# First attention: groups of four heads, one score matmul per block, rough scores by parts of a PSUM bank, and a new order of work

## The chip, the core and the metric

One core of a Trainium2 chip runs the whole kernel in one launch. The metric is the device time in microseconds (us), as the median of several runs. Engines are named TensorE (PE, with its weight loads PEld), VectorE (DVE), ScalarE (ACT), GpSimd (POOL) and SyncE (SP), which only issues DMAs here.

## The reference

Two transformer layers on x (2 x 512 x 128) with a context of 154 rows: an attention with 16 heads of 8, a mixture of experts that picks tokens per expert, a masked attention over the context, and a mixture of experts with 32 experts. Only the first attention is touched. Its input is the layer-normed x, its keys and values come from the context, and it has no mask:

```python
q = (query @ Wq.T + bq).reshape(b, tq, 16, 8).transpose(0, 2, 1, 3)
k = (key @ Wk.T + bk).reshape(b, tk, 16, 8).transpose(0, 2, 1, 3)
v = (value @ Wv.T + bv).reshape(b, tk, 16, 8).transpose(0, 2, 1, 3)
scores = jnp.einsum('bhqd,bhkd->bhqk', q, k) / np.sqrt(8)
attn = jax.nn.softmax(scores, axis=-1)
out = jnp.einsum('bhqk,bhkd->bhqd', attn, v)
out = out.transpose(0, 2, 1, 3).reshape(b, tq, 128)
return out @ Wo.T + bo
```

After it come x1 = x + attention, the gate's scores of x1 (8 experts) and a search for each expert's 128th largest score.

## The kernel before, in words

The kernel is written without a scheduler: each engine has one list of instructions, in the order of the program text, and every hand-over is a semaphore (`wait_ge` ahead of an instruction, `then_inc` behind one). An engine whose next instruction waits does nothing else meanwhile. PSUM has eight banks of 512 float columns, and the text assigns them by hand.

The first attention runs over four combinations c of a batch half b = c // 2 (512 queries) and a half g = c % 2 of the heads (eight heads, 64 rows). The queries and keys stand as rows: keys of a combination are spread over 2 x 616 columns (four heads x 154 keys each, padded to 640), where a head's rows are nonzero only in its own columns (`expand`, by GpSimd, L322, the first by VectorE, L459). So one matmul over 128 key columns scores several heads at once, and 10 blocks of 128 columns make a combination.

For the float precision that is wanted, a query q and a key k are split into high and low parts of type fp32r. The rows are q high and q low (`qa`) against k high twice (`ka`), and q high against k low (`kb`, `qb`). The last rows of `kb` and `qb` hold an indicator of the head (loaded by a DMA of its own, `ind`, and cast at L852) and minus the row maximum, so that the block comes out of PSUM ready for the exponential. A block is thus two matmuls (L1152, 128 rows, and L1153, 72 rows) and one exponential on ScalarE (L868), written into a ring of 8 tiles (`pT`).

The row maximum comes from rough scores (high parts of the keys only), computed ahead: for each tile i of 128 queries, `rough` (L1122) fills three banks (0 to 2; for the first combination 3 to 5 as well) with 512 + 512 + 232 columns, and VectorE reduces 2 x 4 heads x 154 columns at once (L474). `maxima` on TensorE turns the four tiles of maxima (L1047), and ScalarE writes minus the maxima (L815).

`queries(c)` is a full-precision projection into bank 6 (L1088, two passes of 512 columns); ScalarE copies it twice (L801 and L802) and VectorE takes the low part (L465). Bank 6 is also used by `turned`, `values`, `back_turned` and `project`, one after the other. `attend(c, r)` (L1166), r = 0 to 2, multiplies four blocks with the values, as four 32-column groups side by side. `outputs` copies the result (L826), `out_turned` turns it (L1047), `normalise` divides (L487, L488), `back_turned` and `project` (L1209) bring it to x1 (L496). `gate_turn` and `logits` (L1226) begin the gate; `gate_shift` on VectorE (L513 to L520) and `gate_exp` on ScalarE (L841) follow.

The order on TensorE is a loop over c and the ten blocks: score block i, then whatever is due at that i (a rough tile at i = 1, 3, 5, 7 for the next combination, an attend at i = 5, and so on); after the tenth block attend 1, maxima of c + 1, queries of c + 2 and attend 2. In the last combination `logits(0)` stands at i = 8, ahead of attends 1 and 2. ScalarE's list has, behind the last exponential, `gate_exp(0)` and then the two halves of `outputs(3)`. Between them TensorE does matmuls without use (`early_work`, L1066, and `idle_work`, L1053). GpSimd's expansions of combinations 2 and 3 wait for all scores of the combination two before, whose columns they overwrite.

Of the kernel before, what the change touches and what calls it, by code (L numbers as in the profile page):

```python
# [27 lines left out]
COMBOS = 2 * B  # L28
E0, F0 = 8, 512
# [7 lines left out]
for _u in range(PAIRS):  # L37
    STEPS.append((_u, 1))
    if _u + 3 < PAIRS:
# [6 lines left out]
ROUGH_AT = (1, 3, 5, 7)  # L46
ORDER = (0, 3, 5, 8, 1, 4, 6, 9, 2, 7)
ROUNDS = (((0, 0, 0), (1, 1, 1), (2, 0, 2), (3, 1, 3)),
          ((0, 1, 4), (1, 2, 5), (2, 1, 6), (3, 2, 7)),
          ((0, 2, 8), (1, 0, 8), (2, 2, 9), (3, 0, 9)))  # L50
# [18 lines left out]

PACK = {}  # L70
_at = 0
for _name, _width in (("ident", P), ("headmask", HH), ("bq", 2), ("bk", 2), ("vmask", 6 * 2 * DH), ("vones", 6 * 2 * DH), ("tri", P), ("group", P),
                      ("iota", P), ("jf", len(SHIFTS)), ("jg", EXACT + 1), ("cand0", 1), ("bo", D), ("bv", 1),
                      ("ln_w", 1), ("ln_b", 1), ("bd_s", 1), ("b1", E0 * FT), ("esel", E0), ("row", 1)):
    PACK[_name] = (_at, _at + _width)
    _at += _width
# [4 lines left out]
def build(nc, x_d, ctx2_d, mask_d, watt_d, ind_d, pack_d, rows_d, gate_d, fc1_d, fc2_d, wout_d, wr_d, rec_d,  # L81
          bd_d, out_d):
    with ExitStack() as ctx:
# [31 lines left out]
        watt = sb("watt", [P, 6, D])  # L115
# [18 lines left out]
        qa, qb, ka, kb = lay(arena_a, ([P, 2, S], [P, 2, S], [P, 2, NBLK * P], [P, 2, NBLK * P]))  # L134
# [10 lines left out]
        ind = pT[HW:HW + HH, :, :].rearrange("p a b -> p (a b)")[:, 0:NBLK * P]  # L145
# [32 lines left out]
        kT = sb("kT", [P, 2, B, SK])  # L178

        arena_e = sb("arena_e", [P, 2 * E0 * D], F32R)  # L180
        khi, klo = lay(arena_e, ([P, 2, B, SK], [P, 2, B, SK]))
        ohi, olo = lay(arena_e, ([P, E0, D], [P, E0, D]))
        smax = sb("smax", [P, COMBOS * TB, HH])
# [45 lines left out]
        L = {n: sem("ld_" + n) for n in ("x0", "x1", "ctx2", "watt", "pack", "late", "rows", "gate", "fc1", "fc2", "mask", "wout", "wr", "bd", "ind")}  # L229
        names = """var_ready rstd_ready consts_ready xn_ready xnT_psum xnT_ready q_psum qhi_ready qlo_ready k_psum  # L230
        kT_ready khi_ready klo_ready ka_first kb_ind expanded v_psum vraw_ready vaug_ready rough_done max_done twice_var twice_ready
# [21 lines left out]
        def heads(v):  # L253
            return v.rearrange("p (q c) -> p q c", q=2)[:, :, 0:HALF].rearrange("p q (h k) -> p q h k", h=HH // 2)

        def own_heads(rows):
            return const("headmask")[0:rows, :].rearrange("p (q h) -> p q h", q=2)[:, :, :, None]\
                .broadcast_to([rows, 2, HH // 2, SK])
# [3 lines left out]
        def _(sp):  # L262
            sp.dma_start(x[:, 0:TB], x_d[:, 0:TB]).then_inc(L["x0"], 16)
            sp.dma_start(watt[:, 0:4], watt_d[:, 0:4]).then_inc(L["watt"], 16)
            sp.dma_start(watt[:, 4:], watt_d[:, 4:]).then_inc(L["late"], 16)
# [23 lines left out]
        def _(pool):  # L289
# [23 lines left out]
            pool.wait_ge(Z["pad_zero"], 2)  # L313
            expansions = [0]

            def expand(dst, src, c, rows):

                b, g = c // 2, c % 2
                expansions[0] += 1
                if expansions[0] > 1:  # L320
                    pool.wait_ge(Z["expanded"], expansions[0] - 1)
                pool.tensor_tensor(heads(dst[0:rows, c % 2, :]),  # L322
                                   f32(src[0:rows, g, b, None, None, :]).broadcast_to([rows, 2, HH // 2, SK]),
                                   own_heads(rows), ALU.mult).then_inc(Z["expanded"], 1)
# [12 lines left out]

            pool.wait_ge(Z["klo_ready"], 1)
            expand(kb, klo, 0, HW)
            expand(ka, khi, 1, P)  # L340
            expand(kb, klo, 1, HW)
            pool.wait_ge(Z["expanded"], 3)
            pool.wait_ge(L["late"], 48)
            values(0)
            rsqrt()
            indicators(pool.tensor_copy, 1)
            for c in range(2, COMBOS):
                pool.wait_ge(Z["score_psum"], (c - 1) * NBLK)
                expand(ka, khi, c, P)
                expand(kb, klo, c, HW)  # L350
                if c == 2:
                    values(1)
                    pool.wait_ge(L["x0"], 16)
                    pool.wait_ge(L["x1"], 16)
                    pool.tensor_tensor(x1[:, :, :], x[:, :, :], const("bo")[:, None, :].broadcast_to([P, T, D]),
                                       ALU.add).then_inc(Z["xbo_ready"], 1)
# [50 lines left out]
        def _(dve):  # L407
# [40 lines left out]
            def norm(src, dst, t0, done):  # L448
# [5 lines left out]
            dve.wait_ge(Z["kT_ready"], 2)  # L454
            dve.tensor_copy(khi[:, :, :, :], kT[:, :, :, :]).then_inc(Z["khi_ready"], 1)
            dve.wait_ge(Z["khi_ready"], 1)
            dve.tensor_tensor(klo[:, :, :, :], kT[:, :, :, :], f32(khi[:, :, :, :]), ALU.subtract)\
                .then_inc(Z["klo_ready"], 1)
            dve.tensor_tensor(heads(ka[:, 0, :]), f32(khi[:, 0, 0, None, None, :]).broadcast_to([P, 2, HH // 2, SK]),  # L459
                              own_heads(P), ALU.mult).then_inc(Z["ka_first"], 1)  # L460

            def q_lo(c):

                dve.wait_ge(Z["qhi_ready"], 2 * c + 2)
                dve.scalar_tensor_tensor(qa[HW:P, c % 2, :], bank[HW:P, 6, :], const("bq")[HW:P, c % 2:c % 2 + 1],  # L465
                                         f32(qa[HW:P, c % 2, :]), ALU.add, ALU.subtract)\
                    .then_inc(Z["qlo_ready"], 1)

            def maxima(c, i):

                n = c * TB + i
                c0 = 3 * 512 * (i % 2) if c == 0 else 0
                dve.wait_ge(Z["rough_done"], n + 1)
                dve.tensor_reduce(smax[:, n, :].rearrange("p (q h) -> p q h", q=2), heads(flat[:, c0:c0 + NBLK * P]),  # L474
                                  AX.X, ALU.max).then_inc(Z["max_done"], 1)
# [22 lines left out]
            q_lo(0)  # L498
            for i in range(TB):
                maxima(0, i)  # L500
            dve.wait_ge(L["x1"], 16)
            norm(x, xn, TB, "xn_ready")
            dve.wait_ge(L["late"], 48)
            dve.tensor_copy(trib[:, :], const("tri")).then_inc(Z["consts_ready"], 1)
            dve.tensor_copy(groupb[:, :], const("group")).then_inc(Z["consts_ready"], 1)

# [27 lines left out]

            q_lo(1)
            for c in range(COMBOS):
                if c + 1 < COMBOS:
                    for i in range(TB):
                        if c and i == 2:
                            normalise(c - 1)  # L540
                        maxima(c + 1, i)
                    if c + 2 < COMBOS:
                        q_lo(c + 2)
# [235 lines left out]
        def _(act):  # L779
# [71 lines left out]
            for n in range(2):  # L851
                act.copy(kb[HW:HW + HH, n, :], ind).then_inc(Z["kb_ind"], 1)  # L852
            act.wait_ge(L["late"], 48)
            indicators(act.copy, 0)
            for r in range(2):
                values(0, r)
# [834 lines left out]
```

## Time and profile before

| what | value |
|---|---|
| median of 3 runs | 281.58 us (281.22 to 281.99) |
| the profiled execution | 282.88 us |
| its span, first to last instruction | 281.1 us |
| mean granted clock of TensorE | 0.961 |
| busy: PE, PEld, DVE, ACT, POOL | 245.8, 168.1, 180.1, 133.4, 72.5 us |

The profiled execution is one run with the hardware profiler; the trace's times count from the span's start, and 1.8 us lie around the span. A matmul's busy time runs to the modelled end of its results, so neighbours overlap; the distance between starts is what TensorE's queue pays.

### The profile page before, as it was taken

The page shows a single profiled execution, that of the slowest core. Times are in us where ns is not written, and L with a number is a line of the kernel's source. Part 1 is how long each engine was busy: PE and PEld are TensorE (multiplying, and loading weights), DVE is VectorE, ACT ScalarE, POOL GpSimd, SP SyncE. Part 2 cuts the span into 40 slices and gives each one's busy share as a digit, 9 for nine tenths or more (in the row PEclk, how much of TensorE's full clock was granted, in tenths as well). Part 3 has the DMA queues.
Part 4 walks back from the last instruction along what each step waited for, and adds up shares of the span by engine and source line. Part 5 has one row for each costly group of instructions (what it writes and reads, how often), then busy time and mean ns, then how long its engine had stood idle before and what let it go on. Part 6 is the DMA issues. An engine that isn't in the chain of part 4 may idle for free.

```text
span 281.1 us, 3672 instructions
## 1 busy us (share of the span) xinstructions
PE 245.8 (87%) x1244; PEld 168.1 (60%) x1244; DVE 180.1 (64%) x416; ACT 133.4 (47%) x268; POOL 72.5 (26%) x103
## 2 busy tenths in 40 slices
PE   8886998989987666999999768788879999999993
PEld 3454545455644213678788537666558888888872
DVE  3695445363455886677245173688888888888883
ACT  2544364645632940252434233766555555555551
POOL 4572060920305300000192030030023535353200
PEclk9999899999999797799999986999999999999998
DMA  7980000000000000000043000000002121210001
GB/s 244 426 336 3 2 0 0 1 2 1 2 0 0 0 0 2 1 0 0 2 92 100 0 0 0 2 0 1 0 2 61 51 71 44 75 39 0 2 0 75
DMA packets 5156, 11.52 MB, mean 41 GB/s; under 512 B 809, under 2 KB 1929, under 8 KB 4882
## 3 DMA queue, kind: packets, MB, share of 16 engines
q1 hardware_dynamic: 4290, 10.47, 11.3%
q10 hardware_dynamic: 848, 0.82, 0.9%
q8 instruction: 10, 0.16, 0.3%
q14 instruction: 8, 0.07, 0.1%
HBM read 10.77 MB, written 0.52 MB: 40 GB/s over the span
## 4 chain that ended last, share of the span: by engine, by line
PE 65%; DVE 16%; issue 7%; ACT 6%; POOL 5%; DVEq 0%; ACTq 0%; POOLq 0%
PE bank L1517 5%; PE bank L1521 5%; PE bank L1518 5%; PE bank L1047 4%; PE bank L1122 3%; DVE att L571 3%; PE bank L1550 3%; PE bank L1393 3%; PE bank L1066 3%; DVE smax L474 3%; PE bank L1403 3%; PE bank L1547 3%; PE bank L1166 2%; PE bank L1530 2%; PE bank L1548 2%
## 5 line engine op out<-in xcount | busy, mean ns | idle before, releaser
L1012 ACT ACTIVATE arena_d<-bank,bias 128x512 f32<-128x512 f32 x34 | 23.4, 688 | 32.9 <-PE bank L1521 32.9
L868 ACT ACTIVATE arena_c<-bank 128x512 f32<-128x512 f32 x40 | 23.0, 598 | 23.0 <-PE bank L1153 22.9
L474 DVE TENSOR_REDUCE smax<-bank 128x8 f32<-128x1232 f32 x16 | 22.8, 1439 | 15.6 <-PE bank L1122 15.6
L736 DVE SCALAR_TENSOR_TENSOR arena_d<-bank,bias,arena_d 128x512 f32<-128x512 f32 x34 | 25.5, 750 | 10.3 <-ACT arena_d L1012 10.0
L1517 PE MATMUL bank<-arena_b 128*128 128x512 f32 x68 | 27.0, 397 | 0.3 <-DVE arena_d L745 0.3
L1521 PE MATMUL bank<-arena_b 128*128 128x512 f32 x68 | 26.6, 390 | 0.0
L1518 PE MATMUL bank<-arena_b 128*128 128x512 f32 x68 | 26.5, 390 | 0.0
L391 POOL CAST arena_b<-rec 128x512 fp32r<-128x512 f32 x17 | 13.7, 808 | 48.7 <-PE bank L1550 48.6
L297 POOL TENSOR_TENSOR rstd<-vareps,neghalf 128x4 f32<-128x4 f32 x8 | 8.1, 1010 | 62.5 <-DVE vareps L433 62.5
L750 DVE TENSOR_TENSOR arena_a<-arena_d,arena_a 128x512 fp32r<-128x512 f32 x34 | 23.4, 689 | 0.7 <-ACT arena_a L1019 0.7
L633 DVE TENSOR_SCALAR arena_a<-bank,pack 128x512 fp32r<-128x512 f32 x16 | 12.0, 751 | 17.0 <-PE bank L1385 16.9
L1019 ACT CAST arena_a<-arena_d 128x512 fp32r<-128x512 f32 x34 | 20.8, 611 | 3.6 <-DVE arena_d L745 2.3
L745 DVE TENSOR_TENSOR arena_d<-arena_d,bank 128x512 f32<-128x512 f32 x32 | 21.8, 680 | 0.8 <-PE bank L1530 0.8
L322 POOL TENSOR_TENSOR arena_a<-arena_e,pack 64x1232 fp32r<-64x1232 f32 (+1 forms) x7 | 16.7, 2392 | 17.6 <-PE bank L1153 13.4
L1053 PE MATMUL bank<-pack,onesb 128*128 128x512 bf16 x69 | 19.6, 429 | 0.0
L1122 PE MATMUL bank<-arena_a 128*128 128x512 f32 (+1 forms) x48 | 13.8, 400 | 5.8 <-DVE smax L474 3.2
L1152 PE MATMUL bank<-arena_a 128*128 128x512 f32 x40 | 18.3, 458 | 0.3 <-ACT arena_c L868 0.2
L394 POOL TENSOR_TENSOR arena_b<-rec,arena_b 128x384 fp32r<-128x384 f32 x17 | 16.4, 962 | 1.4
L1122 PEld LDWEIGHTS bank<-arena_a 128*128 128x128 f32 x48 | 8.2, 196 | 14.1 <-DVE smax L474 7.2
L1153 PE MATMUL bank<-arena_a 72*128 72x512 f32 x40 | 16.1, 402 | 0.0
L1550 PE MATMUL bank<-arena_a,arena_b 128*128 128x512 f32 x34 | 13.8, 407 | 2.3 <-DVE arena_a L750 2.2
L1517 PEld LDWEIGHTS bank<-arena_b 128*128 128x128 f32 x68 | 12.8, 188 | 3.5 <-DVE arena_d L745 0.7
(247 smaller groups left out, 517.9 us busy)
## 6 DMA issues: line engine op xcount, KB each, us to landing
rec<-in_rec SPq DMA_DIRECT2D x17, 257.0 KB, 2.7
arena_d<-in_fc SPq DMA_DIRECT2D x1, 2048.0 KB, 11.0
fc<-in_fc SPq DMA_DIRECT2D x1, 2048.0 KB, 15.3
x<-in_x SPq DMA_DIRECT2D x2, 256.0 KB, 4.5
out<-x SPq DMA_DIRECT2D x2, 256.0 KB, 2.0
pack<-in_pack ACTq DMA_DIRECT2D x1, 382.0 KB, 5.0
ctx<-in_ctx ACTq DMA_DIRECT2D x2, 154.0 KB, 8.4
watt<-in_watt SPq DMA_DIRECT2D x1, 256.0 KB, 4.1
```

The lines of the kernel that those rows point to most:

```text
L474: dve.tensor_reduce(smax[:, n, :].rearrange("p (q h) -> p q h", q=2), heads(flat[:, c0:c0 + NBLK * P]), AX.X, ALU.max).then_inc(Z["max_don ...
L736: dve.scalar_tensor_tensor(to[:, k % 2, :], bank[:, 2 + k % 2, :], bias[:, u % SPLITS, 1:2], sil[:, k % 2, :], ALU.add, ALU.mult).then_inc ...
L745: dve.tensor_tensor(hh[:, k % 2, :], gu[:, k % 2, :], bank[:, 5 - k % 2, :], ALU.mult)\
L750: dve.tensor_tensor(hlo[:, k % 2, :], hh[:, k % 2, :], f32(hhi[:, k % 2, :]), ALU.subtract)\
L868: act.activation(pT[:, n % RING, :], bank[:, 3 + n % 2, :], ACT.Exp, scale=float(DH) ** -0.5)\
L1012: act.activation(sil[:, k % 2, :], bank[:, k % 2, :], f, bias=bias[:, STEPS[k][0] % SPLITS, 0:1])\
L1019: act.copy(hhi[:, k % 2, :], hh[:, k % 2, :]).then_inc(Z["hhi_ready"], 1)
L1122: ins = pe.matmul(flat[:, c0 + k0:c0 + k1], qa[:, c % 2, i * P:(i + 1) * P], ka[:, c % 2, k0:k1], start=True, stop=True)
L1517: pe.matmul(d, whi[:, r, w], y3hi[:, cs], start=True, stop=False)
L1518: pe.matmul(d, wlo[:, r, w], y3hi[:, cs], start=False, stop=False)
L1521: ins = pe.matmul(d, whi[:, r, w], y3lo[:, cs], start=False, stop=True)
L1550: pe.matmul(d, whi[:, r, w], hlo[:, k % 2, :], start=False, stop=(k == LAST[b]), skip_group_check=True)\
```

## The change

The heads go by four ("quads": QW = 32 rows, cc = 0 to 7, two to a combination). The rows of a quad are q high, q low, q high (`qs`) against k high, k high, k low (`ks`), and four rows with minus the maxima against the indicators: 100 rows in all (KQ), so a block is one matmul. The indicators come out of the expansion itself (ones in the last rows of `kh`), and the DMA of `ind` and its casts are gone. `qs` has 6 slots, `ks` one for each of the 8 quads, so nothing is overwritten. The weights of the queries and keys stand three times in 96 columns per quad, so their DMA is 384 KB instead of 256.

Rough scores take all 96 rows. For quad 0 they go as two parts of two query tiles each (616 columns a tile); for the others a pair of tiles is three parts, each in a bank of its own: 462 columns of the one tile, 462 of the other, and 154 of both (two matmuls). VectorE reduces each part by itself. The loops are replaced by lists written out, for TensorE, VectorE and ScalarE. The logits of half 0 move behind the last attend; `gate_exp(0)` keeps its place ahead of `outputs(3)`. GpSimd has new memsets, expands in order without a wait for scores, and does the second `values` last.

Cut to its core (what isn't shown is the same with other names):

```diff
-ROUGH_AT = (1, 3, 5, 7)
-ORDER = (0, 3, 5, 8, 1, 4, 6, 9, 2, 7)
+ORDER = ((3, 4, 1, 0, 2, 8, 5, 9, 6, 7),
+         (0, 3, 9, 5, 8, 6, 7, 1, 4, 2),
+         (0, 3, 5, 1, 9, 6, 8, 2, 4, 7),
+         (0, 3, 8, 5, 6, 4, 1, 9, 7, 2))
...
-            for v in (ka, kb):
-                pool.memset(v[:, :, :].rearrange("p n (q c) -> p (n q) c", q=2)[:, :, HALF:].bitcast(F32), 0.0)\
-                    .then_inc(Z["pad_zero"], 1)
+            pool.memset(kh[:, :, :, :].bitcast(F32), 1.0).then_inc(Z["pad_zero"], 1)
+            pool.memset(ks[:, :, HALF:].bitcast(F32), 0.0).then_inc(Z["pad_zero"], 1)
+            pool.memset(smax[:, :, :], 0.0).then_inc(Z["pad_zero"], 1)
...
+            for cc in (1, 2, 3):
+                expand(cc)
+            rsqrt()
             pool.wait_ge(L["late"], 48)
             values(0)
-            rsqrt()
             indicators(pool.tensor_copy, 1)
-            for c in range(2, COMBOS):
-                pool.wait_ge(Z["score_psum"], (c - 1) * NBLK)
-                expand(ka, khi, c, P)
-                expand(kb, klo, c, HW)
+            for cc in range(4, QUADS):
+                expand(cc)
...
+            def queries(cc):
+                act.wait_ge(Z["q_psum"], cc + 1)
+                act.activation(qs[0:3 * QW, cc % QSLOTS, :], bank[0:3 * QW, 6, :], ACT.Identity,
+                               bias=const("bq")[0:3 * QW, cc % 4:cc % 4 + 1]).then_inc(Z["qhi_ready"], 1)
...
+            def minus_max(cc):
+                r0, turns = (0, cc) if cc < 2 else (cc % 2 * QW, 1 + cc // 2)
+                act.wait_ge(Z["mT_psum"], turns + 1)
+                act.mul(qs[3 * QW:KQ, cc % QSLOTS, :], bank[r0:r0 + HQ, 7, :], -1.0).then_inc(Z["mT_ready"], 1)
...
+            def rough(cc, part):
...
+                    before = maxes(cc, part - 3) if part > 2 else maxes(cc - 1, part + 3) if cc > 1 else maxes(0, 1)
+                    pe.wait_ge(Z["max_done"], before)
+                    pair, kind = divmod(part, 3)
+                    if kind < 2:
+                        ins = one(bank[:, kind, 0:3 * SK], 2 * pair + kind, 0, 3 * SK)
+                    else:
+                        for t in range(2):
+                            ins = one(bank[:, 2, t * SK:(t + 1) * SK], 2 * pair + t, 3 * SK, HALF)
...
-                pe.matmul(bank[:, 3 + n % 2, :], ka[:, c % 2, cols], qa[:, c % 2, :], start=True, stop=False)
-                pe.matmul(bank[:, 3 + n % 2, :], kb[0:HW + HH, c % 2, cols], qb[0:HW + HH, c % 2, :],
-                          start=False, stop=True).then_inc(Z["score_psum"], 1)
+                pe.matmul(bank[:, 3 + n % 2, :], ks[0:KQ, cc, j * P:(j + 1) * P], qs[0:KQ, cc % QSLOTS, :],
+                          start=True, stop=True).then_inc(Z["score_psum"], 1)
```

The beginning and the end of TensorE's new list (quad, part or combination, block in brackets):

```diff
+            queries(0)
+            keys(2)
...
+            early_work(4, 0)
+            rough(0, 0)
+            keys(3)
+            rough(0, 1)
+            queries(1)
+            pe.wait_ge(Z["max_done"], 1)
+            early_work(4, 0)
+            maxima(0)
+            queries(2)
+            rough(1, 0)
+            rough(1, 1)
+            scores(0, 0)
+            rough(1, 2)
+            rough(1, 3)
+            scores(0, 1)
+            scores(0, 2)
+            values(0, 0)
+            rough(1, 4)
+            rough(1, 5)
+            scores(0, 3)
+            values(0, 1)
+            rough(2, 0)
+            scores(0, 4)
+            turned(1)
+            rough(2, 1)
+            maxima(1)
+            queries(3)
...
+            scores(3, 9)
+            attend(3, 1)
+            attend(3, 2)
+            logits(0)
             pe.wait_ge(Z["consts_ready"], 6)
             for part in range(2):
                 last_out_turned(part)
```

## Rows read from the trace of the kernel before

**Rows 1.** Busy time of each engine in the stage, one window: start:end, length, engines, clock, DMA.

```profile
12.38:79.75 67.37, 60.51 (x319) 34.37 (x319) 34.16 (x59) 36.05 (x65) 23.51 (x23) 0.97 0.12 47
```

**Rows 2.** Groups of instructions, forms apart: busy us, mean ns | idle before, releaser.

```profile
L868 ACT ACTIVATE arena_c<-bank 128x512 f32<-128x512 f32 x40 | 23.0, 598 | 23.0 <-PE bank L1153 22.9
L474 DVE TENSOR_REDUCE smax<-bank 128x8 f32<-128x1232 f32 x16 | 22.8, 1439 | 15.6 <-PE bank L1122 15.6
L322 POOL TENSOR_TENSOR arena_a<-arena_e,pack 64x1232 fp32r<-64x1232 f32 x4 | 10.0, 2500 | 4.1 <-DVE arena_e L457 3.9
L465 DVE SCALAR_TENSOR_TENSOR arena_a<-bank,pack,arena_a 64x512 fp32r<-64x512 f32 x4 | 3.0, 756 | 6.9 <-ACT arena_a L802 6.9
L802 ACT ACTIVATE arena_a<-bank,pack 64x512 fp32r<-64x512 f32 x4 | 2.7, 670 | 0.0
L791 ACT ACTIVATE kT<-bank,pack 128x308 f32<-128x308 f32 x2 | 1.0, 517 | 2.1 <-PE bank L1073 2.1
L519 DVE TENSOR_REDUCE small<-lg 128x4 f32<-128x32 f32 x1 | 0.2, 186 | 0.0
```

**Rows 3.** Two neighbouring windows (columns as in rows 1; the clock is third from the end).

```profile
22.90:26.40 3.50, 1.78 (x8) 1.17 (x7) 2.33 (x7) 1.78 (x4) 0.00 (x0) 1.00 0.00 0
26.40:29.90 3.50, 2.89 (x10) 2.24 (x10) 1.99 (x2) 1.23 (x3) 0.00 (x0) 0.56 0.02 5
```

**Rows 4.** TensorE's timeline at the end of combination 2: start us, us, instruction.

```profile
65.28 0.40 PE L1152 MATMUL bank<-arena_a 128*128 128x512 f32 x1
65.52 0.40 PE L1153 MATMUL bank<-arena_a 72*128 72x512 f32 x1
65.85 1.06 PE L1166 MATMUL bank<-arena_c 128*32 128x512 f32 x8
66.85 0.60 PE L1047 MATMUL bank<-pack,smax 128*8 128x128 f32 x4
67.38 1.06 PE L1166 MATMUL bank<-arena_c 128*32 128x512 f32 x8
68.37 0.51 PE L1152 MATMUL bank<-arena_a 128*128 128x512 f32 x1
68.72 0.40 PE L1153 MATMUL bank<-arena_a 72*128 72x512 f32 x1
```

**Rows 5.** Pieces of the chain of work that ended last: start us, us, what.

```profile
6.91 0.53 PE bank L1073 x2
...
21.79 0.86 PE bank L1088 x2
...
76.40 0.86 PE bank L1226 x8
...
79.75 0.38 ACT osb L826
```

**Rows 6.** VectorE's timeline: the first four maxima, and one in combination 0.

```profile
13.26 5.48 DVE L474 TENSOR_REDUCE smax<-bank 128x8 f32<-128x1232 f32 x4 [0.93 <-PE bank L1122]
...
34.99 1.44 DVE L474 TENSOR_REDUCE smax<-bank 128x8 f32<-128x1232 f32 x1 [0.93 <-PE bank L1122]
```

**Rows 7.** GpSimd's timeline: its last early memset and the first rstd.

```profile
1.42 0.98 POOL L309 MEMSET rows<- 128x1056 f32 x1
5.20 1.01 POOL L297 TENSOR_TENSOR rstd<-vareps,neghalf 128x4 f32<-128x4 f32 x1 [2.80 <-DVE vareps L433]
```

**Rows 8.** The page: DMA traffic in 40 slices of 7.03 us, and the weights' DMA.

```profile
GB/s 244 426 336 3 2 0 0 1 2 1 2 0 0 0 0 2 1 0 0 2 92 100 0 0 0 2 0 1 0 2 61 51 71 44 75 39 0 2 0 75
...
watt<-in_watt SPq DMA_DIRECT2D x1, 256.0 KB, 4.1
```

**Rows 9.** Timeline: the first exponential, the logits, the gate's exponential.

```profile
21.82 0.60 ACT L868 ACTIVATE arena_c<-bank 128x512 f32<-128x512 f32 x1 [0.85 <-PE bank L1153]
...
76.24 1.02 PE L1226 MATMUL bank<-gate,xnT 128*128 128x8 f32 x8
...
78.36 0.22 ACT L841 ACTIVATE lg<-lg 128x32 f32<-128x32 f32 x1
```

More of the change, by code:

```diff
@@ L496, in residual @@
                 dve.tensor_tensor(v, bank[:, 4 if c0 else 6 + b, c0:c1], v, ALU.add).then_inc(Z["x1_ready"], 1)
[L498 to L505, printed above, removed]
+            k_lo(0)
+            dve.wait_ge(Z["klo_ready"], 1)
+            dve.wait_ge(Z["pad_zero"], 3)
+            dve.tensor_tensor(*expansion(0)).then_inc(Z["k_first"], 1)
+            k_lo(1)
             def logit_bank(b):
@@ L887, in _ @@
+            exponents(3, 5)
+            exponents(3, 6)
+            exponents(3, 7)
+            exponents(3, 8)
+            exponents(3, 9)
+            gate_input(0)
             gate_exp(0)
@@ new lines, in _ @@
+            values(0, 1)
+            rough(2, 0)
+            scores(0, 4)
+            turned(1)
+            rough(2, 1)
+            maxima(1)
+            queries(3)
+            rough(2, 2)
+            scores(0, 5)
+            rough(2, 3)
+            scores(0, 6)
+            rough(2, 4)
+            rough(2, 5)
+            scores(0, 7)
+            queries(4)
+            scores(0, 8)
+            rough(3, 0)
+            rough(3, 1)
+            scores(0, 9)
+            rough(3, 2)
@@ new lines, in _ @@
+            attend(0, 0)
+            rough(3, 3)
+            rough(3, 4)
+            rough(3, 5)
+            queries(5)
+            rough(4, 0)
+            attend(0, 1)
+            rough(4, 1)
+            maxima(2, both=True)
+            rough(4, 2)
+            rough(4, 3)
+            rough(4, 4)
+            scores(1, 0)
+            scores(1, 1)
+            attend(0, 2)
+            scores(1, 2)
+            rough(4, 5)
+            scores(1, 3)
+            rough(5, 0)
+            rough(5, 1)
@@ new lines, in _ @@
+            scores(1, 4)
+            queries(6)
+            scores(1, 5)
+            rough(5, 2)
+            scores(1, 6)
+            rough(5, 3)
+            rough(5, 4)
+            attend(1, 0)
+            scores(1, 7)
+            scores(1, 8)
+            rough(5, 5)
+            queries(7)
+            maxima(4, both=True)
+            attend(1, 1)
+            rough(6, 0)
+            rough(6, 1)
+            scores(1, 9)
+            rough(6, 2)
+            scores(2, 0)
+            out_turned(0)
@@ new lines, in _ @@
+            rough(6, 3)
+            scores(2, 1)
+            scores(2, 2)
+            rough(6, 4)
+            values(1, 0)
+            rough(6, 5)
+            attend(1, 2)
+            rough(7, 0)
+            scores(2, 3)
+            scores(2, 4)
+            rough(7, 1)
+            values(1, 1)
+            rough(7, 2)
+            scores(2, 5)
+            rough(7, 3)
+            rough(7, 4)
+            scores(2, 6)
+            out_turned(1)
+            scores(2, 7)
+            rough(7, 5)
```

496 lines of the change are left out of this document (283 added, 213 removed).

## Prediction

> **What bounds the kernel now.** The profiled execution took 282.9 us with a span of 281.1; the median of the runs is 281.6, so 1.3 us are taken off at the end. A difference of 0.3% (0.8 us) is about what a measurement of this kernel can tell from none. The change touches only the first attention, so I cut that stage out of the trace as one window, from the first rough scores at 12.38 to 79.75, where ScalarE copies the last attention output: of 67.4 us TensorE is busy 60.5, ScalarE 36.1 and VectorE 34.2 [rows 1]. Then what the other two waited for, in the groups of instructions: ScalarE idled 22.9 us ahead of exponents for score matmuls and VectorE 15.6 us ahead of maxima for rough scores, so both are followers [rows 2]. Two windows of 3.5 us show one more loss: TensorE is busy 1.78 of 3.5 us, and in the next the granted clock is 0.56, so mostly the lower level, 1.2 GHz; half of those 3.5 us less is about 1.5 us [rows 3].
>
> Busy times of TensorE include the drain of each matmul, so I take starts. Matmuls of 512 columns start 0.24 apart (65.28, 65.52), 0.235 as a mean of such pairs; after an attend or a wait the first takes 0.35, since its weights are loaded in the open; an attend (four pairs side by side) takes 1.00, four turns 0.53 with the open load, so 0.45 without [rows 4]. A query projection takes 0.86, and so do the logits' eight small matmuls with a weight load each, 0.108 apiece; I take 0.86 for every such set of four tiles [rows 5].
>
> TensorE's work in the stage before: 80 score matmuls x 0.235 = 18.8; 16 rough tiles of 1256 columns, 0.6 each by columns, 9.6; 12 attends x 1.1 (with the open load behind) = 13.2; 3 queries 2.6; values, projection and logits 3.8; ten sets of turns 4.5; 11 idle-work matmuls 2.6; together 55.1. The other 12.3 of 67.4 are waits and the slow clock. They are what a new order can win.
>
> **The change, part by part.**
> *One score matmul per block.* 40 x 0.235 = 9.4 us leave TensorE. I take the price of the one left (100 rows) as 0.235, since those of 72 and of 128 rows stand alike [rows 4].
> *Heads by four.* Queries are projected 8 times, not 4: four more x 0.86 = 3.4 on TensorE; keys 4 times, two more x 0.53 [rows 5], of which one before the stage.
> *Rough scores.* The columns are the same (32 x 616 against 16 x 1256), the matmuls 64 against 48. A part of 462 columns is 0.21 by columns; two of 154 cost between 0.14 (columns) and 0.22 (0.108 apiece); the latter, as weights set it. Seven groups of four heads x 6 parts x 0.22 = 9.2, plus 1.3 for the first group (eight matmuls, by columns and 0.108): 10.5, 0.9 more.
> *Turns of maxima.* 5 sets, not 4: 0.5. *Idle work*: 7 fewer behind 12.38: -1.6.
> Logits(0) goes behind the last attend and is counted below: -0.9. TensorE's sum: 55.1 - 9.4 + 3.4 + 0.5 + 0.9 + 0.5 - 1.6 - 0.9 = 48.5.
> *VectorE.* 16 reductions of 1232 elements, back to back 1.37 apart (5.48 for four), become 2 such, 28 of 462 and 14 of 308 elements [rows 6]. Bounds of a small one: by elements alone 0.51 and 0.34; with all of 1.44 kept, 1.44. I take the slope between 1232 and 32 elements (1439 and 186 ns), 1.04 ns per element, the nearest rows of this operation [rows 2], which leaves 0.09 fixed between starts: 0.57 and 0.41. Sum 2.7 + 16.0 + 5.7 = 24.4 against 21.9. In busy time, 0.07 more apiece, that is 27.4 against 23.0. Low parts of the queries: four more x 0.76 = 3.0 [rows 2]; of the keys, two more behind 12.38, at 308 of 512 columns 0.5 each. On the 34.2 busy now [rows 1]: 42.6, all of it beside TensorE's 48.5. VectorE comes near, but isn't the bound; without that cover each part would cost its length.
> The Trainium skill's VectorE: DVE Perf Modes, section on the TRN2 errata, speaks against this step: many small tiles pay a fixed cost each, and it advises tiles of 512 elements or more. Its table's 120 cycles for a PSUM source would make the 28 more reductions dearer by 3.5 us (an estimate from the page), against 2.5 by the row; both leave VectorE under TensorE's sum.
> *ScalarE.* Loses the second copy of each query (0.67 x 4) and the casts of the indicators (not counted), gains four queries (0.67 by the copy's row), four sign changes (0.6, as an exponent) and two keys (0.52): +3.4 [rows 2]. On the 36.1 busy now [rows 1] that is 39.5, hidden under TensorE's 48.5; with that cover gone it would cost all of itself.
> *GpSimd and DMA.* Eight expansions of 616 elements replace those of 1232 at 2.50 [rows 2]; at half, 1.25 each, one of them VectorE's. The seven wait for keys only, no longer for scores, and with the second rstd, values and indicators between them end near 30; the last is read near 47, and TensorE's list up to rough(7) is their cover. New memsets (1232 and 288 elements, at the 0.98 per 1056) put GpSimd's last memset off from 2.4 to near 4, before its first rstd at 5.2 [rows 7]. On SP's queue the first weights grow by 128 KB: at the 244 to 426 GB/s of the first slices they land 0.3 to 0.5 after the 5.3 at which they land now, 4.1 behind their issue [rows 8]; the keys behind them start at 6.91, held by idle matmuls [rows 5]. Every later load of that queue moves by as much, and the first needed of these, the late weights, has over 10 us to spare. The indicators' 40 KB leave ACT's queue, to nobody's cost or gain.
>
> **Walking the new order by hand.** With the durations above I went through the three hand-written lists. (a) Opening: rough(0,0) no longer waits for ScalarE's second copy (0.67, of which 0.6 was exposed): 11.8. Maxima(0) no longer wait for two value sets; first exponent at 18.5, not 21.82 [rows 9]: 3.3 won. Left there are about 0.9 of waits, for k_lo(3) and q_lo(1). (b) From 19 to 24 the values and turned(1) alternate with exponents: 1.9 of waits. (c) After that rough parts fill the places where TensorE waited for a 1.44 reduction plus 0.93 from end to start [rows 6]; three banks give each part three reductions' time. Waits 1.2, and exponent (0,8) stands 1.4 behind attend(0,0) on ScalarE, which no one feels. (d) Each of some 20 short waits opens a weight load of 0.1: 2.0. Waits in all 6.0. Last attend ends at 11.8 + 48.5 + 6.0 = 66.3.
> (e) **A new wait.** Before, logits(0) ran before the last attends: logits 76.24, gate exponent 78.36, output copy 79.75, straight after the last attend [rows 5, 9]. Now logits(0) follows attend(3,2), but ScalarE's list still has the gate exponent ahead of the output copy. The copy pays logits, VectorE's gate shift and the exponent: from 76.24 to 78.58, 2.35. Copy at 66.3 + 2.35 = 68.65, against 79.75: 11.1 us earlier. Everything behind it is untouched and moves along, so 282.9 - 11.1 = 271.8 for a profiled execution, 281.6 - 11.1 = **270.5** for the median.
>
> **Rivals.**
> 1. *Waits stay as large as before.* The new list waits 12.3, not 6.0, because each in-order wait for a small reduction or a bank opens a load and delays exponents. For it: three engines now hand over 44 parts, not 16. Against: TensorE has three banks and scores between. 270.5 + 6.3 = 276.8. Chance 0.12.
> 2. *Nearly no waits left.* Copy at 60.3 + 2 + 2.35 = 64.7: 15.1 won, 266.5. Chance 0.1.
> 3. *The clock falls again.* With 7 idle matmuls fewer and waits near 19 to 24, a stretch at 1.2 GHz like that at 26.4 comes back: +1.5 to 3, 272 to 273.5. Against: TensorE's list is 90% full, where before it was busy 1.78 of 3.5 us ahead of the fall [rows 3]. Chance 0.13.
> 4. *Slower: the reductions' handshake is not hidden.* If a small reduction can't start until 0.93 after the last, as now between tiles [rows 6], because the rough part for it stands in TensorE's list behind a score or an attend that itself waits, 42 x 0.93 = 39.1 go on VectorE's 42.6: copy at 11.8 + 81.7 = 93.5, 13.7 later than now, 295.3. It decides from (79.75 - 11.8 - 42.6) / 42 = 0.60 per part on. Against: three banks, and rough parts spread one or two between scores. Chance 0.03.
> 5. *Nothing comes of it:* TensorE's saved matmuls turn into waits for ScalarE or VectorE one for one, 281.6. Against: neither's queue holds over 40 of the 67 us. Chance 0.02.
> The forecast itself has 0.60.
>
> **How the numbers follow.** The time is that of the forecast. Low end: rival 2 and 0.5 us for my durations, 266.0; high end: rival 1, 276.8, which takes in rival 3 and the dear ends of small matmuls and reductions (2 us at most). Faster 0.95, same 0.02, slower 0.03.
>
> **What would show it.** First exponent near 18.5; the first exponent of combination 1 near 35 and of combination 2 near 46; 40 score matmuls 0.235 apart; small reductions of 0.64 and 0.48 long, 0.57 and 0.41 apart; TensorE's granted clock at 1.00 from 12 to 66; a gap on ScalarE of over 2 us between last exponent and output copy, released by the gate's chain. The forecast is wrong if VectorE's reductions run gapless through the stage (it is then the bound), if the small ones are over 0.8 long, or if the stage behind the copy changes its length by over 1 us.

## The result, and the profile after

The changed kernel takes 269.54 us (268.30 to 269.61, 4 runs) against 281.40 (280.98 to 281.99, 4 runs) for the kernel before: ratio 0.960, 95% interval 0.956 to 0.964. That is 11.9 us faster; forecast was 270.5 in a range of 266.0 to 276.8. The profiled execution took 269.61 with a span of 267.8. Medians, here and below, are of all executions of a kernel, while ratios leave out executions in a slower state of the chip with a lower granted clock, so a ratio is not always the quotient of the two medians beside it.

First the stage in one view, cut at the first rough scores, the first exponential of each combination, and the output copy of combination 3 (windows of the changed kernel; length, busy time of PE, PEld, DVE, ACT, POOL, then clock, DMA share, GB/s).

```profile
11.99:18.92 6.93, 6.17 (x27) 3.63 (x27) 6.31 (x16) 2.84 (x6) 2.61 (x3) 1.00 0.98 389
18.92:35.36 16.44, 16.10 (x83) 9.53 (x81) 14.70 (x29) 10.70 (x21) 9.74 (x11) 1.00 0.10 37
35.36:45.64 10.28, 10.28 (x59) 5.30 (x59) 6.87 (x13) 8.17 (x15) 0.00 (x0) 1.00 0.00 1
45.64:56.58 10.94, 10.88 (x72) 6.55 (x70) 8.50 (x19) 8.10 (x17) 1.43 (x4) 1.00 0.01 1
56.58:67.85 11.27, 10.12 (x68) 5.07 (x66) 3.90 (x19) 7.21 (x15) 2.51 (x5) 1.00 0.01 1
sum 55.86, PE 53.55 PEld 30.08 DVE 40.27 ACT 37.03 POOL 16.29; mean PE 10.71 PEld 6.02 DVE 8.05 ACT 7.41 POOL 3.26
```

The stage is 55.86 us long, not 67.37 [rows 1]. TensorE is busy 96% of it, where it was 90% (2.3 us idle instead of 6.9; 1.1 of the 2.3 lie behind the last attend), and the granted clock is 1.00 throughout: the stretch at 0.56 [rows 3] is gone. VectorE went from 34.2 to 40.3 busy, ScalarE from 36.1 to 37.0.

The instructions that answer to rows 2 and 9 stand in the groups by form and in the timeline of the changed kernel (start, length, instruction, idle time ahead of it and its releaser):

```profile
L936 ACT ACTIVATE arena_c<-bank 128x512 f32<-128x512 f32 x40 | 22.6, 597 | 7.1 <-PE bank L1286 3.3 <-PE bank L1300 3.1
L501 DVE TENSOR_REDUCE smax<-bank 128x3 f32<-128x462 f32 x28 | 17.1, 634 | 3.6 <-PE bank L1241 3.4
L501 DVE TENSOR_REDUCE smax<-bank 128x2 f32<-128x308 f32 x14 | 6.6, 474 | 1.8 <-PE bank L1241 1.8
L346 POOL TENSOR_TENSOR arena_a<-arena_e,pack 100x616 fp32r<-100x616 f32 x7 | 8.4, 1215 | 7.8 <-DVE arena_e L475 7.8
L482 DVE SCALAR_TENSOR_TENSOR arena_a<-bank,pack,arena_a 32x512 fp32r<-32x512 f32 x8 | 5.9, 743 | 1.1 <-ACT arena_a L875 0.9
```

```profile
18.92 0.60 ACT L936 ACTIVATE arena_c<-bank 128x512 f32<-128x512 f32 x1
...
26.94 3.18 DVE L501 TENSOR_REDUCE smax<-bank 128x3 f32<-128x462 f32 x6
...
30.27 0.60 ACT L936 ACTIVATE arena_c<-bank 128x512 f32<-128x512 f32 x1 [1.48 <-PE bank L1300]
...
35.36 1.08 ACT L936 ACTIVATE arena_c<-bank 128x512 f32<-128x512 f32 x2
...
45.15 1.08 ACT L936 ACTIVATE arena_c<-bank 128x512 f32<-128x512 f32 x2
```

The first exponential starts at 18.92 instead of 21.82. From there to the first exponential of combination 1, at 35.36, it is 16.44 us (18.17 before). That of combination 2 is the second of the two at 45.15 and starts at 45.64, so combination 1 takes 10.28 us (15.10 before); combination 2 takes 10.94 (14.06 before), up to 56.58. What was idle is now work: ScalarE waited 23.0 us ahead of its exponentials and waits 7.1; VectorE waited 15.6 ahead of its maxima and waits about 5.8. Six reductions of a group run back to back in 3.18.

Where the stage ends, the new wait stands (timeline of the changed kernel):

```profile
63.80 1.92 PE L1300 MATMUL bank<-arena_c 128*32 128x512 f32 x16
65.66 1.06 PE L1360 MATMUL bank<-gate,xnT 128*128 128x8 f32 x8
66.82 0.19 DVE L538 TENSOR_TENSOR lg<-bank,lg 128x32 f32<-128x32 f32 x1 [3.42 <-PE bank L1360]
...
67.72 0.23 ACT L916 ACTIVATE lg<-lg 128x32 f32<-128x32 f32 x1 [2.74 <-DVE lg L542]
67.85 0.63 ACT L901 COPY osb<-bank 128x256 f32<-128x256 f32 x2
68.35 1.09 PE L1167 MATMUL bank<-pack,osb 128*128 128x128 f32 x4 [1.64 <-ACT osb L901]
```

The last attend is done at 65.7; the copy of its result waits behind the gate's exponential until 67.85, and TensorE stands still for 1.64 us. Behind that its clock falls, which it did not do there before (windows of 3.5 us):

```profile
66.00:69.50 3.50, 1.80 (x11) 1.34 (x10) 1.18 (x6) 0.77 (x3) 0.00 (x0) 0.82 0.00 0
69.50:73.00 3.50, 3.15 (x13) 2.57 (x14) 2.18 (x10) 0.95 (x2) 0.00 (x0) 0.50 0.00 0
73.00:76.50 3.50, 3.28 (x20) 2.79 (x20) 1.81 (x13) 1.17 (x2) 1.68 (x2) 0.70 0.00 0
```

The stretch between the copy and the first count of the threshold search, in the kernel before and in the changed one:

```profile
79.75:91.45 11.70, 8.73 (x56) 5.84 (x56) 7.14 (x31) 3.61 (x9) 4.00 (x7) 1.00 0.00 0
67.85:80.56 12.71, 10.87 (x55) 8.10 (x56) 6.40 (x31) 3.61 (x10) 4.00 (x7) 0.73 0.00 0
```

It is 1.0 us longer now, lost at 1.2 GHz. From that count to the end the changed kernel is 2.4 us shorter in these two executions (187.24 against 189.65, at a mean clock of 0.98 against 0.95): its own stretches at the lower clock fell differently. The execution before lay 1.5 us over the median of its kernel, this one 0.1 over, and no run here shows that this difference comes from the change.

### The profile page after: what moved, and what is told of

Read it like the earlier page. It is cut to its first block, busy times and chain, and to the rows that moved or that the text cites. A ratio compares the mean times of both kernels' runs of the same rounds, so it can differ in the third digit from the quotient of the medians.

```text
span 267.8 us, 3680 instructions
## 1 busy us (share of the span) xinstructions
PE 236.1 (88%) x1216; PEld 163.5 (61%) x1225; DVE 184.5 (69%) x450; ACT 134.3 (50%) x272; POOL 65.4 (24%) x104
## 3 DMA queue, kind: packets, MB, share of 16 engines
q1 hardware_dynamic: 4290, 10.61, 11.6%
## 4 chain that ended last, share of the span: by engine, by line
PE 72%; DVE 17%; ACT 6%; issue 3%; POOL 1%; DVEq 0%; ACTq 0%; POOLq 0%
PE bank L1742 5%; PE bank L1739 5%; PE bank L1738 5%; PE bank L1167 5%; PE bank L1300 4%; PE bank L1286 4%; DVE att L645 4%; PE bank L1241 4%; PE bank L1771 3%; PE bank L1624 3%; PE bank L1768 3%; PE bank L1193 3%; PE bank L1614 3%; PE bank L1751 3%; PE bank L1769 3%
## 5 line engine op out<-in xcount | busy, mean ns | idle before, releaser
L501 DVE TENSOR_REDUCE smax<-bank 128x3 f32<-128x462 f32 (+2 forms) x44 | 25.4, 619 | 5.9 <-PE bank L1241 5.6
L1738 PE MATMUL bank<-arena_b 128*128 128x512 f32 x68 | 27.2, 400 | 0.3 <-DVE arena_d L819 0.3
L1742 PE MATMUL bank<-arena_b 128*128 128x512 f32 x68 | 27.0, 397 | 0.0
L1739 PE MATMUL bank<-arena_b 128*128 128x512 f32 x68 | 26.9, 396 | 0.0
L707 DVE TENSOR_SCALAR arena_a<-bank,pack 128x512 fp32r<-128x512 f32 x16 | 12.0, 751 | 16.0 <-PE bank L1606 13.3
L1241 PE MATMUL bank<-arena_a 96*128 96x462 f32 (+3 forms) x64 | 17.7, 358 | 0.4 <-DVE smax L501 0.3
L1286 PE MATMUL bank<-arena_a 100*128 100x512 f32 x40 | 17.7, 468 | 0.0
L1173 PE MATMUL bank<-pack,onesb 128*128 128x512 bf16 x64 | 17.1, 399 | 0.6 <-issue 0.4
L410 POOL TENSOR_TENSOR arena_b<-rec,arena_b 128x384 fp32r<-128x384 f32 x17 | 16.4, 964 | 1.4
L1241 PEld LDWEIGHTS bank<-arena_a 96*128 96x128 f32 x64 | 11.3, 189 | 8.2 <-issue 3.7
L1738 PEld LDWEIGHTS bank<-arena_b 128*128 128x128 f32 x68 | 12.9, 190 | 3.5 <-DVE arena_d L819 0.8
L1742 PEld LDWEIGHTS bank<-arena_b 128*128 128x128 f32 x68 | 13.0, 191 | 2.8
L1739 PEld LDWEIGHTS bank<-arena_b 128*128 128x128 f32 x68 | 12.9, 190 | 2.6
```

The costliest lines, as they stand in the source:

```text
L501: dve.tensor_reduce(dst, src, AX.X, ALU.max).then_inc(Z["max_done"], 1)
L1241: return pe.matmul(to, qs[0:3 * QW, cc % QSLOTS, t * P:(t + 1) * P], ks[0:3 * QW, cc, k0:k1], start=True, stop=True)
L1286: pe.matmul(bank[:, 3 + n % 2, :], ks[0:KQ, cc, j * P:(j + 1) * P], qs[0:KQ, cc % QSLOTS, :], start=True, stop=True).then_inc(Z["score_psu ...
L1738: pe.matmul(d, whi[:, r, w], y3hi[:, cs], start=True, stop=False)
L1739: pe.matmul(d, wlo[:, r, w], y3hi[:, cs], start=False, stop=False)
L1742: ins = pe.matmul(d, whi[:, r, w], y3lo[:, cs], start=False, stop=True)
```

## The experiments

The four of the first group were timed in 3 rounds together, beside a kernel before of 282.16 us. The output copy's start in the trace is the sharper reading, since it stands in one stage. In the changed kernel it is at 67.85, and at 67.43 in a second execution of it, timed with the second group. The two differ as much already at the first exponential (18.92 and 18.50); from there to the copy both take 48.93 us. So a copy read by itself is good to about 0.4 us, and its distance from the first exponential is sharper.

**All score matmuls twice.**

```diff
-                pe.matmul(bank[:, 3 + n % 2, :], ks[0:KQ, cc, j * P:(j + 1) * P], qs[0:KQ, cc % QSLOTS, :],
-                          start=True, stop=True).then_inc(Z["score_psum"], 1)
+                for again in range(2):
+                    ins = pe.matmul(bank[:, 3 + n % 2, :], ks[0:KQ, cc, j * P:(j + 1) * P], qs[0:KQ, cc % QSLOTS, :],
+                                    start=True, stop=True)
+                ins.then_inc(Z["score_psum"], 1)
```

> The changed kernel with every score matmul issued twice into the same bank (the second overwrites the first, so the result is unchanged). Theory: TensorE's list bounds the stage, so 40 x 0.235 = 9.4 us come back nearly in full: 277.5 to 279 us, output copy at 76 to 77.5 instead of 67.85. Rival (hand-overs to VectorE or ScalarE bound the stage): less than 4 us come back, below 273.5.

275.84 us (ratio to before 0.983, interval 0.975 to 0.992); output copy at 74.35, 6.5 later. Of 9.4 us of TensorE's work 6.5 show, two thirds; both the time and the copy lie below the theory's range. The other 2.9 must have fitted where TensorE's next start was late anyway; its idle time hardly shows it (2.0 us from 12.00 to the copy, 2.3 in the changed kernel), because busy time counts the drain of each matmul. TensorE's list is the main bound, but less alone than the theory had it; the rival's 4 is out.

**The 14 smaller reductions twice**, the extra one into a spare tile:

```diff
+                if cc and part % 3 == 2:
+                    k = 2 * (2 * (cc - 1) + part // 3)
+                    spare = work[:, :, :, :].rearrange("p a b c -> p (a b c)")[:, k:k + 2]
+                    dve.tensor_reduce(spare, src, AX.X, ALU.max)
                 dve.tensor_reduce(dst, src, AX.X, ALU.max).then_inc(Z["max_done"], 1)
```

> The changed kernel with the 14 reductions over 308 elements done twice (the extra one writes a spare tile): 5.7 us more on VectorE's list. Theory: VectorE has about 5 us to spare before its last maximum, so at most 2 us show: 269.5 to 271.5. Rival (VectorE bounds the stage): all 5.7 show, 275.

273.00 us (0.973, 0.962 to 0.985); output copy at 70.48, 2.6 later. Neither number came: the median is above the theory's 271.5 and below the rival's 275, and at the copy it is more than the theory's 2 and less than half of the rival's 5.7. The copies of the earlier combinations tell where: from 38.67 to 40.21 (+1.5) for combination 0, 49.46 to 51.56 (+2.1) for 1, 59.68 to 62.29 (+2.6) for 2. Counted from the first exponential (18.69 here) it is 1.8, 2.3 and 2.9, and 2.9 at the last copy. So most was lost in the first combination. Two runs at the end test that.

**The parts of a group together** in TensorE's list:

```diff
             rough(1, 1)
-            scores(0, 0)
             rough(1, 2)
             rough(1, 3)
+            rough(1, 4)
+            rough(1, 5)
+            scores(0, 0)
             scores(0, 1)
             scores(0, 2)
             values(0, 0)
-            rough(1, 4)
-            rough(1, 5)
...
```

(and so for groups 2 to 7: parts 1 to 5 directly behind part 0.)

> The changed kernel, but in TensorE's list the six rough parts of each group of four heads stand one behind the other, where the first of them stood; all work and VectorE's and ScalarE's lists stay. Theory: the spread of the parts hides the reductions; together, parts 3 to 5 each wait 0.35 to 0.6 us for a reduction, in 7 groups 1 to 2 us each, so +5 to +12 us: 274.5 to 281.5. Rival (the gain is the removed matmuls alone, the place of the parts doesn't matter): below 271.

284.78 us (1.015, 1.007 to 1.024): slower than the kernel before by 1.5%, with the whole new arithmetic in it. The output copy is at 83.89, 16.0 later, and the time is over the 281.5 at the top of the theory's range. The waits in the trace, of this kernel (engine and line, releaser, us in total, times, longest):

```profile
ACT arena_c L936 <- PE bank L1286: 12.5, 9, 3.0
PEld bank L1241 <- DVE smax L501: 10.6, 23, 1.3
PEld bank L1286 <- ACT arena_c L936: 9.6, 16, 1.2
```

and of the changed kernel:

```profile
PEld bank L1286 <- ACT arena_c L936: 4.7, 9, 0.8
ACT arena_c L936 <- PE bank L1286: 3.3, 6, 0.8
PEld bank L1241 <- DVE smax L501: 2.7, 5, 0.8
```

TensorE's weight loads for rough parts wait 23 times for a reduction instead of 5, 7.9 us more, as the theory had it. What I had left out is the second half: while TensorE stands at a part, the scores behind it come late, ScalarE runs dry (12.5 instead of 3.3), and when the scores do come they come in a row and wait for two banks of exponentials (9.6 instead of 4.7). The granted clock also falls twice in this stage (0.87 in the mean of 22 to 35 and of 50 to 63), which is part of the 16 us; why it falls there was not tested.

**The kernel before, one score matmul per block.**

```diff
-                pe.matmul(bank[:, 3 + n % 2, :], ka[:, c % 2, cols], qa[:, c % 2, :], start=True, stop=False)
-                pe.matmul(bank[:, 3 + n % 2, :], kb[0:HW + HH, c % 2, cols], qb[0:HW + HH, c % 2, :],
-                          start=False, stop=True).then_inc(Z["score_psum"], 1)
+                pe.matmul(bank[:, 3 + n % 2, :], ka[:, c % 2, cols], qa[:, c % 2, :], start=True, stop=True)\
+                    .then_inc(Z["score_psum"], 1)
```

> The kernel before with the second score matmul of each block left out (it leaves out query high times key low and the subtraction of the maximum): the work is removed, the old order stays. If removing work is what gave the gain: 40 x 0.235 = 9.4 us, 272. Theory: in the old order many of these matmuls ran while TensorE would have waited for a reduction or an exponential anyway, so only 4 to 7 us come: 274.5 to 277.5.

277.30 us; the interval of the ratio (0.972 to 1.004) takes in no change, but the trace is clear: the output copy stands at 75.56, not 79.75. The waits of this kernel, and its stage in one window:

```profile
ACT arena_c L868 <- PE bank L1152: 19.3, 20, 2.1
DVE smax L474 <- PE bank L1122: 14.1, 13, 2.1
```

```profile
12.38:75.56 63.18, 51.63 (x279) 27.43 (x279) 34.20 (x59) 35.37 (x65) 23.51 (x23) 0.97 0.14 52
```

Of 9.4 us of removed work 4.2 come; ScalarE still waits 19.3 us and VectorE 14.1, nearly as before [rows 2]. TensorE is busy 8.9 us less and stands idle 4.7 us more (11.6 against 6.9 [rows 1]). So in the old order over half of these matmuls ran while TensorE would have waited anyway.

The second group, 5 rounds together, beside a kernel before of 281.54 us, asks about the end of the stage.

**The changed kernel again.**

> The changed kernel itself, to stand beside the three below on the same chip: 269.5 us, output copy of combination 3 at 67.9.

269.32 us (0.959, 0.955 to 0.964), output copy at 67.43, first count of the search at 80.1.

**Output copies ahead of the gate's exponential**, in ScalarE's list:

```diff
             gate_input(0)
-            gate_exp(0)
             for c0, c1 in ((0, S // 2), (S // 2, S)):
                 outputs(COMBOS - 1, c0, c1)
+            gate_exp(0)
```

> The changed kernel with ScalarE's two output copies of combination 3 ahead of the gate's exponential (two lines exchanged). Theory: the copy starts 2.1 us earlier (65.8), but TensorE turns it only behind the logits and VectorE normalises only behind its gate shift, so 1.3 us come from that; the pause of TensorE shrinks, and if its clock no longer falls behind it another 1.0: 267.2 to 268.4. Rival (something else ends last there, such as the gate's scores): no gain, 269.5.

267.49 us (0.953, 0.949 to 0.958), inside the theory's range. The timeline and two windows of this kernel:

```profile
65.34 0.65 ACT L901 COPY osb<-bank 128x256 f32<-128x256 f32 x2 [0.81 <-PE bank L1300]
```

```profile
66.00:69.50 3.50, 2.47 (x16) 1.52 (x15) 2.66 (x12) 1.18 (x3) 0.00 (x0) 1.00 0.00 0
69.50:73.00 3.50, 3.17 (x23) 2.40 (x24) 2.50 (x14) 1.17 (x2) 0.84 (x1) 1.00 0.00 0
```

The copy is 2.1 earlier than in the run beside it, released by the attend; the clock stays at 1.00, and the search begins at 77.9, 2.2 earlier than 80.1. The median shows 1.8 of that. The intervals of the two ratios, this one and 0.955 to 0.964 of the changed kernel, overlap a little; the start of the search is the sharper reading, here and in the next two runs.

**Idle matmuls in the pause**, nothing else moved:

```diff
             logits(0)
             pe.wait_ge(Z["consts_ready"], 6)
+            idle_work(6, 3)
             for part in range(2):
                 last_out_turned(part)
```

> The changed kernel with six matmuls without use (1.3 us) between the logits and the turns of the last output, where TensorE stands still for 1.6 us; nothing else moves. Theory: the pause is what lets the granted clock fall to 0.50 behind it, and the fall costs 1.0 to 1.5 us: with the pause filled the clock stays at 1.00 there and the time is 268.0 to 268.6. Rival (the fall comes from something else or costs nothing, or is only put off): 269.3 to 269.8.

267.16 us (0.952, 0.947 to 0.956), a little better than the theory said; single times spread from 266.8 to 272.1. The profiled execution took 270.57, 3.4 over the median, so I read only the part up to the search:

```profile
67.34 0.63 ACT L901 COPY osb<-bank 128x256 f32<-128x256 f32 x2
```

```profile
66.00:69.50 3.50, 2.65 (x14) 1.23 (x16) 1.87 (x10) 0.86 (x4) 0.00 (x0) 1.00 0.00 0
69.50:73.00 3.50, 3.07 (x21) 2.15 (x21) 2.90 (x14) 1.90 (x4) 0.00 (x0) 1.00 0.00 0
```

The copy has not moved, the clock has: 1.00 where the changed kernel had 0.50. The search begins at 79.0, 1.1 earlier than 80.1, 11.7 behind the copy as in the kernel before. So the pause costs twice: its own length, and the clock behind it. The median shows 2.2, the trace 1.1 of them; where the rest comes from is open.

**Logits between the last two attends.**

```diff
-            scores(3, 8)
             gate_turn(0)
+            scores(3, 8)
             scores(3, 9)
             attend(3, 1)
-            attend(3, 2)
             logits(0)
+            attend(3, 2)
...
-            exponents(3, 9)
             gate_input(0)
-            gate_exp(0)
+            exponents(3, 9)
             for c0, c1 in ((0, S // 2), (S // 2, S)):
                 outputs(COMBOS - 1, c0, c1)
+            gate_exp(0)
```

> The changed kernel with the gate's turn ahead of score 8, the gate's input copy ahead of exponent 9, logits(0) between the last two attends, and the output copies ahead of the gate's exponential. Theory: the gate's chain runs beside the last attend and nothing waits for it: output copy at 66.8, turned and normalised at once, 2 us or more gained with the clock: 266.8 to 268. Rival (the added copy delays the last exponent and attend by as much): 268.5 to 269.5.

267.40 us (0.951, 0.947 to 0.956), the middle of the theory's range, and no better than the two exchanged lines: the copy waits 1.95 us for the last attend and starts at 67.02, the clock stays at 1.00 up to the search, which begins at 78.7. The copy is 1.7 later than with the two exchanged lines (1.1 counted from the first exponential), so part of what the rival named is there: the logits and the input copy now stand ahead of the last attend. The clock falls later in this run, inside the search (0.87 in the mean of 80 to 97).

The third group, beside a kernel before of 281.93 us, splits the doubled reductions by place (3 rounds) and tries one step more (5 rounds).

**The early ones twice** (`if 1 <= cc <= 3 and part % 3 == 2:`) and **the late ones twice** (`if cc >= 4 and part % 3 == 2:`).

> The changed kernel with only the six reductions over 308 elements of groups 1 to 3 done twice (2.5 us on VectorE's list; the extra ones write a spare tile). Theory, formed after the doubled maxima cost more than I allowed: VectorE has no time to spare in the first combination, where it is busy 14.7 of 16.4 us, so at least 1.5 of the 2.5 us show: output copy at 69.2 or later, 270.8 to 272. Rival (its spare time is even over the stage, 5 us in 40): under 1.2 show.

> The changed kernel with only the eight reductions over 308 elements of groups 4 to 7 done twice (3.3 us on VectorE's list). Theory: VectorE has its spare time there (busy 7.7 of 11.1 us per combination), so at most 1.2 us show: output copy by 69.1, below 270.8. Rival (spare time even over the stage, or none): 1.5 to 3.3 show, more than in the run with the early ones.

Medians of 270.01 and 269.73 don't tell them apart (0.956, 0.950 to 0.963, and 0.956, 0.950 to 0.961). The output copies of the four combinations do. The early ones:

```profile
39.94 0.58 ACT L905 COPY osb<-bank 128x512 f32<-128x512 f32 x1
50.72 0.59 ACT L905 COPY osb<-bank 128x512 f32<-128x512 f32 x1 [0.57 <-PE bank L1304]
60.93 0.58 ACT L905 COPY osb<-bank 128x512 f32<-128x512 f32 x1
69.11 0.63 ACT L905 COPY osb<-bank 128x256 f32<-128x256 f32 x2
```

and the late ones:

```profile
38.18 0.58 ACT L905 COPY osb<-bank 128x512 f32<-128x512 f32 x1
49.53 0.59 ACT L905 COPY osb<-bank 128x512 f32<-128x512 f32 x1 [0.57 <-PE bank L1304]
60.25 0.58 ACT L905 COPY osb<-bank 128x512 f32<-128x512 f32 x1
68.43 0.63 ACT L905 COPY osb<-bank 128x256 f32<-128x256 f32 x2
```

Against the second execution of the changed kernel (38.27, 49.04, 59.25, 67.43) the early ones cost 1.7 of 2.5 us, all of it before the first copy; the late ones 1.0 of 3.3, half of it in each of the next two combinations. Counted from the first exponential it is 1.7 and 1.1, together the 2.9 of all 14 within 0.1. (The 7.7 of 11.1 us in the expectation is for 35.36 to 46.49, which ends one exponential late; combination 1 has 6.87 of 10.28 and combination 2 has 8.50 of 10.94.) So VectorE is a bound of the first combination beside TensorE, and mostly hidden afterwards. The early copy is at 69.11 where I had named 69.2 or later, and its median (270.01) lies below the 270.8 I had named: the outcome is seen in the stage, not in the whole.

**Output copies first, and six idle matmuls per round of the search** (`idle_work(6, 5)` for `idle_work(5, 5)`).

> The version with the output copies first, and six matmuls without use instead of five in each round of the threshold search, where the granted clock still falls to 0.5 near its end in every run. Theory: the sixth is hidden under VectorE's 1.3 us count and keeps TensorE busier, and if the clock stays at 1.00 the turns, gate positions and gathers behind the search take 1 us less: 266 to 267 against 267.5. Rival (the sixth makes each round wait, or the clock falls all the same): 267.3 to 269.

266.52 us (0.945, 0.940 to 0.950), the fastest of all, 15.4 under the kernel before beside it. In the window 95 to 105 the granted clock is 0.83, with five matmuls 0.67: the fall is smaller, not gone. The sixth matmul is hidden: the eight counts of the search lie as far apart as with five (first to last 14.9 us in both). It ran in another group than the run with five (0.953, 0.949 to 0.958), so the last microsecond between them is likely, not shown.

## Why the prediction was right

**The bound.** That TensorE's list bounds the stage held in the main: doubled scores cost 6.5 of 9.4. The estimate of VectorE ("comes near, but isn't the bound") was right in the main for combinations 1 to 3, where 1.0 of 3.3 added us show, and wrong for combination 0, where it is busy 14.7 of 16.4 us and 1.7 of 2.5 added us show. My sum over the whole stage hid that its work is unevenly laid. It was also too high, 42.6 against 40.3: I added the rise of the reductions' lengths (4.4 us) to a busy time in which overlaps count once, and counted so they rose by 2.6.

**The prices.** Reductions of 462 and 308 elements were put at 0.64 and 0.48 and took 0.634 and 0.474; six in a row, forecast at 0.57 and 0.41 between starts, took 3.18, with 0.55 and 0.39 where no wait lies between. The fixed cost by the slope of two rows held. One sign named in the forecast did not come: score matmuls "0.235 apart". From the start of one to TensorE's next start it is 0.23 to 0.64 us, with a median of 0.33; the 0.235 is the low end, as it was in the kernel before, where only half of the 40 pairs L1152 to L1153 stand under 0.25 apart. Expansions at half of a larger one (1.25) took 1.215, low parts of a query 0.743. ScalarE's sum was 39.5 and came out as 37.0: I had not taken off the two casts of the indicators at 1.25.

**The walk.** First exponential forecast at 18.5, measured 18.92 (18.50 in the second execution); of combination 1 35 and 35.36; of combination 2 46 and 45.64; exponent (0,8) was to stand 1.4 behind attend(0,0) and stood 1.48 (the row at 30.27). The last attend was to end at 66.3 and ended at 65.7: start and work as forecast would leave 65.7 - 12.0 - 48.5 = 5.2 for waits where I had 6.0. Whether the waits were smaller is not shown, since the sum of the work was not measured and the median distance behind a score matmul says that 48.5 may be low. What is shown is that work and waits together are 0.8 less.

**The new wait (e).** It is there as described: 2.15 us from the end of the last attend to the copy (2.35 forecast), the gate's chain its releaser, and it can be taken away (267.49). What I missed is its echo: "everything behind it is untouched and moves along" was wrong, since the clock fell to 0.50 behind the pause, 1.0 us more up to the search; the filled pause shows that cause by itself. The forecast had named a change of over 1 us behind the copy as a sign that it is wrong, and that sign came: 12.71 against 11.70 up to the search, and 199.95 against 201.35 from the copy to the end. I had looked for a fall of the clock (rival 3) in the first combination, where none came.

**The rivals.** *Waits stay as large* and *handshake not hidden* are what the kernel becomes when the parts of a group stand together: copy at 83.89, past the 79.75 of before. So rival 4's mechanism is real, though smaller than its 93.5; the spread of the parts over the list is what keeps it away. In the old order, leaving out one of the two score matmuls brings 4.2 us at the copy; the changed kernel with as many score matmuls put back brings 5.4 (79.75 to 74.35). Neither alone gives the 11.9 at the copy, and the two add up to 9.6: the removal is worth 4.2 in the old list and 6.5 in the new one. So each carries roughly half. The "new list" of this split includes the heads by four, the smaller reductions and the expansions without a wait: the old order with all of the new arithmetic was not built, and only its likeness, the parts together, was.

**The sum.** 68.65 was forecast for the copy and 67.85 came, 0.8 less; 11.1 was forecast for the whole and 11.9 came. That the whole gained just what the copy gained is in part luck: 1.0 of the 11.9 was lost again behind the copy, and the medians still differ by 11.9. Between the two profiled executions it is 13.3 (11.9 at the copy, 1.0 lost, 2.4 won behind the first count), and the forecast has no term for what is won there. Its cause is open.

**The Trainium skill's rule on small tiles** (VectorE: DVE Perf Modes, section on the TRN2 errata) would have made 28 more reductions 3.5 us dearer (the prediction's estimate from the page), the row's slope 2.5. The page of the changed kernel's profile has all 44 in one group:

```profile
L501 DVE TENSOR_REDUCE smax<-bank 128x3 f32<-128x462 f32 (+2 forms) x44 | 25.4, 619 | 5.9 <-PE bank L1241 5.6
```

Their busy time, overlaps counted once, is 25.4 us against 22.8 for the 16 of before [rows 2]: 2.6 more, so the row's slope was the better price. The fixed cost is real here; the order hides most of it, except in combination 0.

## What to carry to other kernels

When engines run fixed lists, removing work from the busiest pays only as far as its waits don't swallow it: here 4.2 of 9.4 us in the old order. Spread small producer steps between others so that each has the time of several consumer steps, and walk the lists by hand with measured distances between starts: that found both the gain and the new wait. Add up an engine's work by stretches and not over the whole stage. Look at what stands in an engine's list ahead of a copy that the next step needs, and at any pause of TensorE there, since the clock behind it can cost again, as it did here.

## What was unexpected of the hardware

A pause of 1.64 us at one hand-over was followed by a granted clock of 0.50, the lower level of 1.2 GHz, from 69.5 to 73 and a mean of 0.70 after it; with the pause filled by idle matmuls, or cut short by the output copies first, it stayed at 1.00 there. A quiet stretch doesn't always bring the fall: from 76.5 to 80 TensorE is busy 1.53 of 3.5 us both in the run with the filled pause and in the one with the earlier logits, and from 80 to 97 the clock is 1.00 in the first and 0.87 in the second. And idle matmuls paid although nothing uses their results: 2.2 us in the median (269.32 to 267.16), of which the trace shows 1.1 up to the search.
